# Four transformer layers on one core: first-layer weights packed into two loads, X's other tiles held back, and VectorE's residual addition ahead of its softmax sums

## The reference

```
q = Wq x + bq;  k = Wk ctx + bk;  v = Wv ctx + bv        # 64 x 64 weights over the 64 rows of a batch
k, v padded by 8 columns left and 7 right; every column t sees a window of 16
attn = softmax(q . k_window / sqrt(8))                   # 8 heads of 8
x = x + Wo (attn . v_window) + bo
# then a feed-forward part with int8-like quantisation: gate and up matmuls, silu, down matmul
```

## Time and profile before

| | |
|---|---|
| median of 3 runs | 1669.07 us (1667.07 to 1669.41) |
| profiled execution, its own time | 1672.39 us |
| its span, first to last instruction | 1670.6 us |
| mean granted TensorE clock | 0.982 of full |
| PE busy | 1577.3 us, 94% |
| VectorE, ACT, POOL busy | 823.0, 754.4, 518.0 us |

### The profile page before, as it was taken

How to read it: one execution, slowest core, us unless ns; L and a number is a source line. 1 busy time by engine, 2 the same in 40 slices (tenths; PEclk the granted TensorE clock), 3 DMA queues, 4 the chain that set the end, 5 groups by cost and what they waited for, 6 DMA issues and landing times. The chain is left out here.

```text
span 1670.6 us, 25988 instructions
## 1 busy us (share of the span) xinstructions
PE 1577.3 (94%) x9522; PEld 1282.7 (77%) x9522; DVE 823.0 (49%) x1697; ACT 754.4 (45%) x2529; POOL 518.0 (31%) x648
## 2 busy tenths in 40 slices
PE   7998998789999999999999998878999999999998
PEld 5877777678888888888888887655555578888876
DVE  3555666445444355554444435765565412333455
ACT  3544444444444454545454555444343211454552
POOL 5666564232222222222222223333232100123333
PEclk8999998999999999999999999998999999999999
DMA  8000000102001010101010110001100000222111
GB/s 237 14 7 7 8 1 14 51 2 95 26 4 47 15 38 26 39 26 39 26 39 26 39 51 1 1 29 51 39 1 1 20 9 11 69 73 74 47 31 60
DMA packets 45678, 58.22 MB, mean 35 GB/s; under 512 B 26368, under 2 KB 33920, under 8 KB 42736
## 3 DMA queue, kind: packets, MB, share of 16 engines
q1 hardware_dynamic: 43872, 56.05, 10.6%
q10 hardware_dynamic: 1616, 0.51, 0.1%
q0 software_dynamic: 64, 0.00, 0.0%
HBM read 48.94 MB, written 2.10 MB: 31 GB/s over the span
## 5 line engine op out<-in xcount | busy, mean ns | idle before, releaser
L1747 ACT ACTIVATE big<-pb 128x128 f32<-128x128 f32 x384 | 106.6, 278 | 312.3 <-PE pb L807 203.0
L2110 POOL TENSOR_TENSOR big<-big 128x512 f32<-128x512 f32 x96 | 99.9, 1041 | 260.9 <-DVE big L1392 260.9
L1798 ACT ACTIVATE big<-pb,big 128x128 f32<-128x128 f32 x384 | 136.1, 368 | 64.3 <-issue 41.6
L1387 DVE TENSOR_REDUCE big<-pb 128x4 f32<-128x512 f32 x96 | 65.8, 686 | 180.0 <-PE pb L846 171.5
L822 PE MATMUL pb<-wkh,CXh 128*128 128x256 f32 x512 | 149.3, 292 | 1.5 <-DVE big L1377 1.5
L822 PE MATMUL pb<-wkl,CXh 128*128 128x256 f32 x512 | 144.3, 282 | 0.0
L822 PE MATMUL pb<-wkh,CXl 128*128 128x256 f32 x512 | 143.6, 281 | 0.0
L2100 POOL TENSOR_SCALAR big<-big 128x6 f32<-128x6 f32 x64 | 13.1, 204 | 419.3 <-ACT big L1747 419.0
L1180 DVE TENSOR_TENSOR X<-X,pb 128x512 f32<-128x512 f32 x128 | 86.9, 679 | 85.5 <-PE pb L1028 41.5
L871 PE MATMUL pb<-woh,oh 128*128 128x512 f32 x256 | 112.6, 440 | 8.0 <-DVE X L1180 5.0
L807 PE MATMUL pb<-wqh,CXh 128*128 128x512 f32 x256 | 102.1, 399 | 5.8 <-DVE big L1357 4.4
(11 more groups left out here) (255 smaller groups left out, 3979.2 us busy)
## 6 DMA issues: line engine op xcount, KB each, us to landing
big<-in_w SPq DMA_DIRECT2D x17, 1024.0 KB, 4.9
big<-in_w SPq DMA_DIRECT2D x24, 256.0 KB, 2.9
big<-in_w SPq DMA_DIRECT2D x8, 512.0 KB, 3.5
o<-o SPq DMA_DIRECT2D x96, 32.0 KB, 1.9
X<-in_x SPq DMA_DIRECT2D x8, 256.0 KB, 7.4
big<-in_cn SPq DMA_DIRECT2D x8, 256.0 KB, 3.1
CXlf<-in_cT SPq DMA_DIRECT2D x8, 256.0 KB, 5.0
big<-in_wa SPq DMA_DIRECT2D x1, 2048.0 KB, 7.9
```

The source lines that it names most:

```text
L1387: v.tensor_reduce(m[j % 2], quarters(bank(p)), AX, MAX, negate=True).then_inc(S.m, 1)
L1747: y = a.activation(sq[i % 2], bank(p)[:, j * width:j * width + 128], ACT.Square, accum_out=ss[i % 2][:, first + j:first + j + 1])
L1798: y = a.activation(e_[:, c], bank(p)[:, c], ACT.Exp, bias=m[j % 2][:, k:k + 1], scale=1.0, accum_out=z[j % 2][:, k:k + 1])
L2110: g.tensor_tensor(quarters(e_), quarters(e_), bc(r[j % 2], 128), MUL).then_inc(*on.to(S.pn))
```

## The change

The twelve loads of ACT become four. `w0` (128 x 394) holds Wq, Wk, Wv, bq, bk and the head mask; `wo_raw` (128 x 134) holds Wo, bv, the other head mask and bo; `band` stays; `pad` has 16 partitions instead of 128, and so have its matmuls. Waits for them become waits for one load each. SP issues the first tile of X and the first context tile, then waits until VectorE has written the first normalised rows (`S.xn` at 1), and issues the identity and all else. POOL's two loads move to `l0_bias`. `l0_bias` moves from behind step 2 to behind step 5. In the list `l0` the stage `l0_out` stands ahead of `l0_sum`; the context splitting of ACT and POOL is now a stage `l0_ctx` at the old place. The places for `together` grow by one. As the other engines have no part in `l0_sum` and `l0_out` but PE in the second and POOL in the first, only VectorE's order of the two changes. Left out below are the renamed semaphores and functions and the parts of the host's packing that only rearrange.

```diff
-    l0 = [("l0_mask", 2), ("l0_rows", 1), ("l0_sum", 4), ("l0_out", 7), ("l0_weigh", 6), ("l0_turn", 5),
+    l0 = [("l0_mask", 2), ("l0_rows", 1), ("l0_out", 7), ("l0_sum", 4), ("l0_ctx", 7), ("l0_weigh", 6), ("l0_turn", 5),
           ("l0_scores", 3), ("l0_project", 2), ("l0_norm", 0), ("l0_qk", 1)]
...
-            together(next(att0), (iter([[("l1_begin", 0)]]), 6), (ffn0, 6), (ffn0, 8))
+            together(next(att0), (iter([[("l1_begin", 0)]]), 7), (ffn0, 7), (ffn0, 9))
         else:
-            together(next(att0), (ffn0, 6), (ffn0, 8))
-        if step == 2:
+            together(next(att0), (ffn0, 7), (ffn0, 9))
+        if step == 5:
             order.append(("l0_bias", 0))
...
-        together(first[:6], (ffn0, 6))
+        together(first[:7], (ffn0, 7))
...
-        wq0, wk0, wv0 = al(128), al(128), al(128)
+        w0 = al(394)
+        wq0, wk0, wv0 = w0[:, 0:128], w0[:, 128:256], w0[:, 256:384]
+        bq0, bk0, hm = w0[:, 384:385], w0[:, 385:386], w0[:, 386:394]
...
-        wob, band = CXf[0][:, 64:192], CXf[0][:, 2048:2688]
+        wo_raw, band = CXf[0][:, 64:198], CXf[0][:, 2048:2688]
+        wob, bv0, hmo, bo_raw = wo_raw[:, 0:128], wo_raw[:, 128:129], wo_raw[:, 129:133], wo_raw[:, 133:134]
...
             def l0_project(u):
-                on.wait_ge(D.wv, 32)
+                on.wait_ge(D.w0, 16)
+                on.wait_ge(D.pad, 16)
...
-                    a = pe.matmul(bank(p)[:, g * 128:g * 128 + 128], pad[:, g // 3 * 128:g // 3 * 128 + 128],
-                                  pad[:, 256:384], start=False, stop=True, skip_group_check=True)
+                    a = pe.matmul(bank(p)[:, g * 128:g * 128 + 128], pad[0:16, g // 3 * 128:g // 3 * 128 + 128],
+                                  pad[0:16, 256:384], start=False, stop=True, skip_group_check=True)
...
             def begin(_):
-                for dst, name, landed in ((wq0, "wq0", D.wqk), (bq0, "bq0", D.wqk), (wk0, "wk0", D.wqk), (bk0, "bk0", D.wqk),
-                                          (band[0:16], "band", D.band), (wv0, "wv0", D.wv), (pad, "pad", D.wv),
-                                          (hm, "hm", D.hm), (bv0, "bv0", D.wo), (wob, "wo0", D.wo), (bo0, "bo0", D.wo),
-                                          (hmo, "hmo", D.wo)):
-                    a.dma_start(dst, d[name]).then_inc(landed, 16)
+                a.dma_start(w0, d["w0"]).then_inc(D.w0, 16)
+                a.dma_start(band[0:16], d["band"]).then_inc(D.band, 16)
+                a.dma_start(pad[0:16], d["pad"]).then_inc(D.pad, 16)
+                a.dma_start(wo_raw, d["wo0"]).then_inc(D.wo, 16)
...
             def begin(_):
-                g.dma_start(qw, d["qw"]).then_inc(D.nw, 16)
-                g.dma_start(kw, d["kw"]).then_inc(D.nw, 16)
                 g.memset(half[:, :], -0.5).then_inc(*on.to(S.zp))
...
+            def l0_bias(_):
+                g.dma_start(qw, d["qw"]).then_inc(D.nw, 16)
+                g.dma_start(kw, d["kw"]).then_inc(D.nw, 16)
...
             def l0_mask(u):
-                on.wait_ge(D.hm, 16)
+                on.wait_ge(D.w0, 16)
...
             def begin(_):
                 load(X[:, 0, :], d["x"][0], D.x[0])
+                load_cn(0)
+
+                on.wait_ge(S.xn, 1)
                 load(ident[:, :], d["ident"], D.ident)
-                load_cn(0)
                 load(X[:, 1, :], d["x"][1], D.x[1])
                 load_cn(1)
...
+    m["w0"] = np.concatenate([diag(i["L0_xattn_Wq"].T), diag(i["L0_xattn_Wk"].T), diag(i["L0_xattn_Wv"].T)[:, order],
+                              bq, bk, heads], 1)
+    m["wo0"] = np.concatenate([diag(i["L0_xattn_Wo"].T)[order], bv[order], heads, bo], 1)
-    m["pad"] = np.zeros((128, 384), np.float32)
+    m["pad"] = np.zeros((16, 384), np.float32)
```

More of the change, by code:

```diff
@@ L399, in build_program @@
         D.ident, D.nw, D.f0, D.ct = sem("d_ident"), sem("d_nw"), sem("d_f0"), sem("d_ct")
-        D.wqk, D.wv, D.band, D.hm, D.wo = sem("d_wqk0"), sem("d_wv0"), sem("d_band"), sem("d_hm"), sem("d_wo0")
+        D.w0, D.pad, D.band, D.wo = sem("d_w0"), sem("d_pad"), sem("d_band"), sem("d_wo0")
         D.wq1, D.wo1, D.kv1, D.w2q, D.mk = sem("d_wq1"), sem("d_wo1"), sem("d_kv1"), sem("d_w2q"), sem("d_masks")
@@ L513, in build_program @@
         wo0 = al(4 * 128).rearrange("p (h n) -> p h n", h=4)
-        bq0, bk0, bo0 = al(1), al(1), al(1)
-        bv0, hm, hmo = al(1), al(8), al(4)
+        bo0 = al(1)
         al = carve(R1 + 6144, R1 + 10240)
         CPt, CP = slots(al, 2, 528), slots(al, 3, 512)
-        wq0, wk0, wv0 = al(128), al(128), al(128)
+        w0 = al(394)
+        wq0, wk0, wv0 = w0[:, 0:128], w0[:, 128:256], w0[:, 256:384]
+        bq0, bk0, hm = w0[:, 384:385], w0[:, 385:386], w0[:, 386:394]
         pad, bandb = al(384), al(640, BF16)
-        wob, band = CXf[0][:, 64:192], CXf[0][:, 2048:2688]
+        wo_raw, band = CXf[0][:, 64:198], CXf[0][:, 2048:2688]
+        wob, bv0, hmo, bo_raw = wo_raw[:, 0:128], wo_raw[:, 128:129], wo_raw[:, 129:133], wo_raw[:, 133:134]
         al = carve(RF, R0 + 22788)
@@ L678, in l0_bias @@
                 p = PSUM["l0_bias", 0, "bo"]
-                on.wait_ge(D.wo, 64)
+                on.wait_ge(D.wo, 16)
                 pe.matmul(bank(p)[:, 0:1], wob, bv0, start=True, stop=True).then_inc(p.full, 1)
@@ L687, in l0_qk @@
                 p = PSUM["l0_qk", u, "q"]
-                on.wait_ge(D.wqk, 64)
+                on.wait_ge(D.w0, 16)
                 rows_made(on, "l0", t)
@@ L1246, in l0_bias @@
                 on.wait_ge(p.full, p.n + 1)
-                v.tensor_tensor(bo0, bo0, bank(p)[:, 0:1], ADD).then_inc(p.free, 1)
+                v.tensor_tensor(bo0, bo_raw, bank(p)[:, 0:1], ADD).then_inc(p.free, 1)
             def l0_norm(u):
@@ L1686, in l0_weigh, with l0_ctx @@
                     a.copy(AV[u % 2][:, h * 512:h * 512 + 512], bank(p)).then_inc(p.free, 1)
-            def l0_out(u):
+            def l0_ctx(u):
                 if 8 <= u < 16:
@@ L1976, in scalar_program @@
             do = dict(begin=begin, l0_bias=l0_bias, l0_qk=l0_qk, l0_project=l0_project, l0_scores=l0_scores, l0_turn=l0_turn,
-                      l0_weigh=l0_weigh, f0_quant=f0_quant, f0_quant_u=f0_quant_u, f0_quant2=f0_quant2, f0_turn=f0_turn, f0_gate=f0_gate, f0_turn2=f0_turn2, l0_out=l0_out, l1_begin=l1_begin, l1_keys=l1_keys, l1_q=l1_q, l1_k=l1_k,
+                      l0_weigh=l0_weigh, f0_quant=f0_quant, f0_quant_u=f0_quant_u, f0_quant2=f0_quant2, f0_turn=f0_turn, f0_gate=f0_gate, f0_turn2=f0_turn2, l0_ctx=l0_ctx, l1_begin=l1_begin, l1_keys=l1_keys, l1_q=l1_q, l1_k=l1_k,
                       l1_b=l1_b, l1_s=l1_s, l1_t=l1_t, l1_v=l1_v, l1_d=l1_d, f1_turn=f1_turn, l2_kv=l2_kv,
@@ L2180, in f3_mm @@
                 g.tensor_tensor(X[:, t, :], X[:, t, :], b3, ADD).then_inc(*on.to(S.xb))
-            do = dict(begin=begin, l0_norm=l0_norm, l0_mask=l0_mask, l0_sum=l0_sum, l0_out=l0_out, f0_norm=f0_norm,
+            do = dict(begin=begin, l0_bias=l0_bias, l0_norm=l0_norm, l0_mask=l0_mask, l0_sum=l0_sum, l0_ctx=l0_ctx, f0_norm=f0_norm,
                       f0_silu=f0_silu, f0_down=f0_down, l1_k=l1_k, l1_z=l1_z, f1_quant=f1_quant, l2_begin=l2_begin, l2_a=l2_a, l2_z=l2_z,
@@ L2393, in diag @@
         return z
-    m["wq0"] = diag(i["L0_xattn_Wq"].T)
-    m["wk0"] = diag(i["L0_xattn_Wk"].T)
     order = np.arange(128).reshape(2, 2, 32).transpose(1, 0, 2).reshape(128)
[L2398 to L2401, removed]
     p = np.arange(128)
-    m["bv0"] = c(np.tile(i["L0_xattn_bv"], 2)[order, None])
-    m["pad"] = np.zeros((128, 384), np.float32)
+    bq, bk, bv, bo = [np.tile(i[f"L0_xattn_b{n}"], 2)[:, None] for n in "qkvo"]
+    heads = ((p[:, None] % 64) // 8 == np.arange(8)[None, :]).astype(np.float32)
+    m["w0"] = np.concatenate([diag(i["L0_xattn_Wq"].T), diag(i["L0_xattn_Wk"].T), diag(i["L0_xattn_Wv"].T)[:, order],
+                              bq, bk, heads], 1)
+    heads = ((p[:, None] % 32) // 8 == np.arange(4)[None, :]).astype(np.float32)
+    m["wo0"] = np.concatenate([diag(i["L0_xattn_Wo"].T)[order], bv[order], heads, bo], 1)
+    m["pad"] = np.zeros((16, 384), np.float32)
     for b in range(2):
```

2 lines of the change are left out of this document (removed).

## The result

| | before | changed |
|---|---|---|
| median | 1669.03 us (1667.07 to 1669.41, 4 runs) | 1651.32 us (1648.66 to 1652.87, 4 runs) |
| profiled execution, its own time | 1672.39 us | 1652.87 us |
| its span | 1670.6 us | 1651.1 us |
| mean granted clock | 0.982 | 0.991 |

The ratio is 0.9895, with a 95% interval of 0.9877 to 0.9912: 17.7 us faster, against 19 forecast. The two profiled executions are 19.5 us apart, against 20.5 in the sum.

The account below looks back on a forecast made before the run. TensorE, busy 94% of the span, was taken as the bound. 5.8 + 4.1 + 4.9 + 6.8 − 1.1 = 20.5 us off 1672.39 gives 1651.9, off the median 1648.6; forecast 1650, range 1645 to 1664.

Parts of the forecast that it names:

- Start, arrival: Start of first layer: packed loads land sooner, first scores at 11.5 instead of 17.34; gain 5.8 us, bounds 5.3 and 6.1.
- Start, clock: First scores and projections: with the wait cut to 0.4 us the clock stays at 2.4 GHz; gain 4.1, ends 0 and 6.0.
- The start as a whole: Start of first layer: earlier first scores, 5.8 us, and the clock staying up there, 4.1, taken together.
- Gate waits: Layer 1 gate matmuls: additions ahead of the sum, 0.88 us sooner at five gates and 0.46 at one; gain 4.9.
- Falls at the gates: Layer 1 gates: with the shorter wait four clock falls go, 1.69 us each; gain 6.8, ends 0 and 6.8.
- The clock rival: Start and gates: the clock does not follow the waits and falls as before; 1659.5 us, chance 0.27.
- End of the layer: Last sum of the first layer starts 1.9 us late against about 0.8 of cover; loss 1.1, ends 0 and 1.9.
- `pad` with 16 partitions: Pad matmuls: same columns, so 0; at best 0.1 us gained on each of 16, 1.6.
- Costs put at 0: SyncE's held-back loads, POOL's two moved loads and the bias stage three steps later were each priced at 0.
- That the swap buys nothing: Gates: another wait takes the place of the removed one, only the start's 5.8 is left; 1663.3 us, chance 0.10.
- That the start is hidden: First layer's pace is set by something with a fixed date; with the swap also lost 1669 us, chance 0.07.
- That the sum becomes the bound: Each of 29 steps' turns is late by the additions' 0.6 us, 17.4 in all; about 1681 us, chance 0.05.

Follow-up runs that it names:

- experiment 1: The changed kernel with VectorE's old order, sum ahead of addition, so the new loads alone: 1660.85 us, ratio 0.9942.
- experiment 3: The changed kernel with the bias stage `l0_bias` back behind step 2: 1654.55 us, ratio 0.9897.
- experiment 8: The changed kernel with its loads unpacked to twelve and `pad` with 128 partitions; swapped order, late bias, SP's wait and POOL's moved loads kept: 1653.51 us, ratio 0.9894.
- experiment 9: The kernel of experiment 8 with VectorE's additions ahead of the normalised rows as well as the sum: 1644.85 us, ratio 0.9839.
- experiment 4: The changed kernel without SP's wait for the first rows, identity and rest of X issued at once: 1653.84 us, ratio 0.9892.
- experiment 5: The changed kernel run again, unedited: 1653.07 us, ratio 0.9891 to the kernel before.
- experiment 6: The changed kernel with VectorE's additions ahead of the normalised rows too: 1644.90 us, ratio 0.9851.
- experiment 2: The kernel before with only `l0_out` ahead of `l0_sum`, twelve loads and bias at step 2 kept: 1661.98 us, ratio 0.9945.
- experiment 10: The kernel of experiment 2 with the bias stage at step 5; loads, SP and POOL as before: 1653.30 us, ratio 0.9885.

## Why the prediction was right, and where its steps were not

**Start, arrival (5.8).** The term was mis-sized, and measured 5.3 at the first scores. The step was "X and w0 now share the engines in their first 3 us". The prediction worked out about 0.4 us from the rows there, and then kept 5.8 as if the rows gave no delay. In the changed kernel's execution X came 0.45 later (4.19 against 3.74). Over all profiled executions the statistics start at 3.99 to 4.19 with packed loads (seven) and at 3.62 to 3.81 without (five). The prediction set the Trainium skill's page "DMA: Bandwidth & Descriptors" (section "Queues, rings and completion order"), by which the engines take turns between the two queues, beside a term of 5.3. The trace agrees, with first scores 5.3 earlier (12.05 against 17.34).

**Start, clock (4.1).** The size is right in the two traces compared, 9.7 − 5.3 = 4.4 at the first `l0_weigh` (26.09, where 26 was forecast). The step was too sure. "I take it that the clock then stays" held in the changed kernel's profiled execution and in those of experiments 1, 3, 8 and 9. It failed in experiments 4 and 5, where the clock fell near 18.5 for 13.7 us, and in experiment 6, where it fell at 18.2 for 3.4 us; PE had waited 0.66 at most since its scores began. The argument "the falls in this layer all come with waits" failed there. That the changed kernel's own profile was one of those that held is luck. And the term is not kept whole: 5.7 us apart at the first gate, the two executions of the same program ended 1.7 apart (experiment 5).

**The start as a whole (9.9).** By medians, experiments 2 and 10 give 17.7 − 9.6 = 8.1 for the late bias alone. The prediction had three waits at the start, for the fourth load, for `hm` and for the twelfth, and took the first scores' date as the gain. Of the three, the wait for the twelfth load carries nearly all of the measured gain, through the clock; the other two are still there in experiment 10, which by the medians is as fast as the changed kernel.

**Gate waits (4.9).** Right: each is 0.83 shorter (2.22 to 1.39) where 0.88 was worked out, the one at 83 us is gone, 4.7 in all by the list of waits (13.7 − 9.0). Experiment 2 has it alone.

**Falls at the gates (6.8).** Right as a step: four of 1.69 were forecast to go, and all four are gone. With the waits of 2.2 put back, they returned at four gates of five (experiment 1). Over all profiled executions, 42 gates that waited 1.02 to 1.40 kept the full clock. The clock rival is refuted for this half.

The last gate lost its fall too (5.41 before, 3.72 after), though its wait of 2.23 stayed. This is not a gain of the change. In nine of the twelve profiled executions the clock falls some 15 us ahead of the last gate (at 277.0 in the changed kernel's) and the gate takes 3.72; in the other three (the kernel before, experiments 3 and 10) it doesn't, and the gate's own matmuls are partly at half clock. Why the fall comes at the one place or the other is not shown. What the sum lacks is a term for falls that move in this way. Between 1080 and 1121 us, in a layer that the edit doesn't touch, the lead shrinks from 22.2 to 20.0 with as many us at half clock as before, but at other instructions.

**End of the layer (−1.1).** This step failed: "The sum then starts near 290.4, 1.9 late, against about 0.8 of cover." The trace after shows:

```profile
270.08 0.29 DVE L1284 TENSOR_TENSOR X<-X,pb 128x128 f32<-128x128 f32 x1 [1.15 <-PE pb L765]
...
270.67 0.68 DVE L1273 TENSOR_REDUCE big<-big 128x16 f32<-128x512 f32 x1
...
271.68 1.11 PE L736 MATMUL pb<-ident,big 128*128 128x128 f32 x4
271.71 1.05 POOL L2062 TENSOR_TENSOR big<-big 128x512 f32<-128x512 f32 x1 [1.83 <-DVE big L1276]
```

The sum is late as said, but the turn at 271.68 starts before POOL has normalised this sum's unit: it reads the unit before. The turn that needs this one comes at 280.79, with 8 us of cover. I had counted the cover to the wrong turn. The lead is 19.7 us at this turn (291.38 to 271.68) and still 19.7 at the last gate, so nothing was lost.

**`pad` with 16 partitions (0 to 1.6 gained).** This came out beyond its bounds: a pair takes 0.48 instead of 0.39 (experiment 8 has 128 partitions in the same start), a loss of 0.09 on each of 16. By starts it is more: the next matmul starts 0.41 after the pair's start, and 0.22 to 0.32 after it with 128 partitions. How much of this reaches the time is not shown.

**Costs put at 0.** SP's wait costs nothing (experiment 4, without it, is no faster), and neither does the bias at step 5 (experiment 3). For POOL's two loads, no wait of PE for POOL appeared in the first layer of the changed kernel.

**Rivals.** That the swap buys nothing is refuted by experiment 2. That the start is hidden is refuted by experiment 1 (10.7 with the order left alone). That the sum becomes the bound is refuted by the list of waits, in which no turn waits for POOL. The clock rival is half true: the start's clock falls in some executions, and then costs less than its price by the end.

**The number.** The forecast median was 1650, measured 1651.3 and 1653.1. That the total came so near is in part luck: the arrival was 0.5 too high, the loss of 1.1 didn't come, the last gate's 1.7 came on top, and behind 1080 us 2.7 of the lead were lost again (22.2 to 19.5).

## What to carry over

Ask of every wait at the start what stands in the list behind the waiting instruction, and first move the consumer that is needed late. Here one number (the step of a bias stage) did as much for the median as the packing of twelve loads, a held-back queue and moved loads. A bank that two stages share is released by an operation on another engine: put that operation ahead of less urgent work there, and also ahead of work that itself waits for a third engine. A gain that rests on the granted clock is to be priced over the whole run and over several executions, since a fall that is taken away at one place can come at another. Compare executions at the same clock before you say that an edit brought nothing.

## What the runs showed of the hardware

- The granted clock can fall to 0.50 with hardly a wait of PE ahead: at 18.5 in one execution of the changed kernel and not at all before 266 in another. Between the first scores and 18.5 PE ran the same instructions in both, scores in pieces of 64 columns and projections, with the same wait, 0.65 in the one and 0.66 in the other.
- Gates with a wait of 1.02 to 1.40 us ahead of them kept the full clock in 42 cases of 42. Gates with a wait of 2.08 to 2.23 us ran partly at half clock in 11 cases of 22: five of six in the kernel before, four of six in experiment 1, and two of the ten last gates of the other kernels.
- A short wait is no safeguard at other places: in experiment 10 the clock fell at 147.1, after waits of 1.54 and 0.73 us ahead of two turns.
- A pair of fp32 matmuls with 16 partitions and 128 columns took 0.48 us, with 128 partitions 0.39.
- A load of 202 KB at the head of ACT's queue, in place of the first of twelve small ones, put the first 256 KB of SP's queue back by 0.2 to 0.6 us (3.99 to 4.19 in seven executions, 3.62 to 3.81 in five). Loads behind it in the same queue (experiment 4) put it back by nothing that shows (4.16 against 4.19).
